# Two matmuls a token group in place of three for head scores and head values, in a two-layer transformer kernel

## What is computed

```python
def _L1_attn_ref(x, Wqkv, Wproj, bproj):
    qkv = jnp.einsum('bnm,fm->bnf', x, Wqkv).reshape(b, n, N_HEADS, -1)
    q, k, v = (qkv[..., :dh], qkv[..., dh:2 * dh], qkv[..., 2 * dh:])
    scores = jnp.einsum('bnhd,bngd->bnhg', q, k) / SCALE
    attn = jax.nn.softmax(scores, axis=-1)
    out = jnp.einsum('bnhg,bngd->bnhd', attn, v).reshape(b, n, -1)
    return jnp.einsum('bni,mi->bnm', out, Wproj) + bproj
```

## Time and profile before

| | us |
|---|---|
| three runs | 1480.59, 1487.53, 1486.54 |
| median | 1486.54 |
| profiled execution | 1478.55 |
| its span | 1476.6 |
| TensorE / VectorE / ScalarE / GpSimd busy | 1193.3 / 944.1 / 659.7 / 576.5 |
| mean granted clock of TensorE | 0.85 of full speed |

### The profile page before, as it was taken

How to read it: one execution, slowest core, us unless ns; L and a number is a source line. 1 busy time by engine, 2 the same in 40 slices (tenths; PEclk the granted TensorE clock), 3 DMA queues, 4 the chain that set the end, 5 groups by cost and what they waited for, 6 DMA issues and landing times.

```text
span 1476.6 us, 31197 instructions
## 1 busy us (share of the span) xinstructions
PE 1193.3 (81%) x12328; PEld 768.5 (52%) x12328; DVE 944.1 (64%) x2129; ACT 659.7 (45%) x1116; POOL 576.5 (39%) x888
## 2 busy tenths in 40 slices
PE   6678888988988888988979888988979877784443
PEld 3444555654655555554655565555655545442332
DVE  3444567586676767487667767487666777474524
ACT  3322472357424672357423762357423672356123
POOL 3125335335524534335524534334523515340312
PEclk8689996899879996899879986899879996797566
DMA  4000280207311280208320380208320290209120
GB/s 170 15 1 15 65 122 2 73 15 154 48 44 32 92 122 2 72 15 157 45 73 8 95 114 2 72 16 161 41 59 1 81 121 2 58 29 161 13 58 29
DMA packets 93017, 90.58 MB, mean 61 GB/s; under 512 B 7046, under 2 KB 81736, under 8 KB 92616
## 3 DMA queue, kind: packets, MB, share of 16 engines
q1 hardware_dynamic: 90312, 80.20, 28.3%
q0 software_dynamic: 2560, 8.39, 1.6%
HBM read 46.62 MB, written 41.94 MB: 60 GB/s over the span
## 4 chain that ended last, share of the span: by engine, by line
PE 41%; DVE 23%; POOL 9%; DMA 8%; issue 7%; ACT 7%; SPq 4%; POOLq 0%; DVEq 0%; ACTq 0%
PE bank L1468 39%; DVE blockdiag L1194 3%; POOL rs L517 3%; DVE keys L1259 3%; DMA bt<-scratch_o 3%; SPq L447 2%; DVE x L1167 2%; DVE gelu L1261 2%; DMA scratch_o<-stage 2%; DVE ct L1001 1%; ACT x L772 1%; DVE stats L1031 1%; DMA scratch_qkv<-part 1%; DMA scratch_qkv<-stage 1%; PE bank L1478 1%
## 5 line engine op out<-in xcount | busy, mean ns | idle before, releaser
L1468 PE MATMUL bank<-we,at 128*128 128x512 f16 x1536 | 368.8, 401 | 1.8 <-DVE x L1167 1.8
L1468 PEld LDWEIGHTS bank<-we,at 128*128 128x128 f16 x1536 | 154.7, 102 | 196.4 <-issue 40.7
L532 POOL TENSOR_TENSOR part<-part 128x512 f32<-128x512 f32 x64 | 82.9, 1295 | 283.0 <-ACTq L798 283.0
L667 ACT ACTIVATE part<-bank,wexp 128x256 f32<-128x256 f32 x256 | 105.2, 469 | 186.4 <-PE bank L1468 128.1
L1167 DVE SCALAR_TENSOR_TENSOR x<-bank,wexp,x 128x256 f32<-128x256 f32 x256 | 122.2, 477 | 72.6 <-PE bank L1468 66.6
L513 POOL TENSOR_SCALAR nm<-mv 128x2 f32<-128x2 f32 x128 | 32.2, 252 | 333.6 <-DVE mv L1036 329.1
L772 ACT ACTIVATE x<-x,nm,rs 128x256 f32<-128x256 f32 x192 | 104.6, 593 | 108.1 <-POOL nm L520 107.0
L1468 PE MATMUL bank<-bt,wqkv 128*128 128x512 f16 x576 | 137.5, 380 | 17.0 <-DVE stage L1001 13.3
L1001 DVE TENSOR_TENSOR stage<-bank,stage 128x512 f16<-128x512 f32 x112 | 75.4, 685 | 83.2 <-ACT stage L667 83.2
L667 ACT ACTIVATE stage<-bank 128x512 f16<-128x512 f32 x112 | 66.1, 597 | 126.8 <-PE bank L1468 73.6
L1468 PE MATMUL bank<-keys,blockdiag 128*128 128x16 f16 x3072 | 96.7, 193 | 26.9 <-DMA keys<-scratch_qkv 18.2
(11 more groups left out here) (177 smaller groups left out, 2241.0 us busy)
## 6 DMA issues: line engine op xcount, KB each, us to landing
scratch_qkv<-stage SPq DMA_DIRECT2D x40, 512.0 KB, 3.8
ct<-scratch_qkv SPq DMA_DIRECT2D x128, 128.0 KB, 6.0
x_in<-in_x_dram SPq DMA_DIRECT2D x32, 256.0 KB, 2.8
keys<-scratch_qkv SPq DMA_DIRECT2D x64, 128.0 KB, 5.4
scratch_o<-stage SPq DMA_DIRECT2D x64, 128.0 KB, 3.1
bt<-scratch_o SPq DMA_DIRECT2D x16, 512.0 KB, 3.8
out_dram<-x POOLq DMA_DIRECT2D x32, 256.0 KB, 2.6
scratch_qkv<-part SPq DMA_DIRECT2D x8, 512.0 KB, 8.4
```

Source lines behind the costliest of these rows:

```text
L532: pool.tensor_tensor(part[:, 0:2, :], part[:, 0:2, :], part[:, 2:4, :], ALU.add)\
L667: return act.activation(dst, src, ACT.Copy, scale=scale)
L1468: ins = pe.matmul(dst, lhs, rhs, start=(n == 0), stop=(n == len(terms) - 1))
```

## The change

- Each token group takes two matmuls in place of three: the HI matrix times 32 columns (HI and LO of keys or probabilities side by side), and the LO matrix times the 16 HI columns, added onto the first 16. A bank then holds two values a score, so quarters become eighths: S0 to S7 and O0 to O7, of 16 groups and 32 matmuls.
- VectorE evicts each of them with a `tensor_reduce` (add, pairs at a distance of 16) into half of `prob` (`b_s`, `b_o`). The maximum and the subtraction (`b_shift`) and the row sum (`b_ssum`) are functions of their own, over quarters, and now read `prob`.
- O's HI (ScalarE) and LO (VectorE, `b_olo`) are taken from `prob` in SBUF, 256 values each, in steps of 128 values, and no longer from PSUM.
- ScalarE makes 6 of V's 16 spreads, four of half 0 and two of half 1. VectorE makes the other ten, in five pieces placed at other points of its list.
- The order lists of all three engines are rewritten around that; ScalarE's normalisation `a_ln2n(b, 0)` comes ahead of the fourth exponent. SyncE's two waits ahead of the store become one. GpSimd's list is as it was.

```diff
+        def products(name):
+            return b_ps(name).rearrange("p (a l g) -> p a g l", l=2, g=H)
+        def prob_half(n):
+            return prob[:, n // 2 % 2, 256 * (n % 2):256 * (n % 2 + 1)]
+        def o_sum(n):
+            return prob_half(n).rearrange("p (c r h) -> p h r c", c=2, r=T)
 
...
-                sp.wait_ge(b_free[b_ring("O2")], b_read(b, "O2"))
-                sp.sem_inc(waits_held, 1)
-                sp.wait_ge(b_free[b_ring("O3")], b_read(b, "O3"))
+                sp.wait_ge(o_lo, 8 * (b + 1))
                 sp.sem_inc(waits_held, 1)
...
-            def b_o(b, q):
-                act.wait_ge(b_full, b_filled(b, f"O{q}"))
-                act.wait_ge(v_spread, 2 * b + 2)
-                copy(o_part(q, HI), o_psum(q)).then_inc(o_hi, 1)
+            def b_o(b, n):
+                for hf in range(2):
+                    act.wait_ge(v_spread[hf], 2 * (b + 1))
+                act.wait_ge(b_free[b_ring(f"O{n}")], b_read(b, f"O{n}"))
+                copy(o_part(n, HI), o_sum(n)).then_inc(o_hi, 1)
+            def b_spreadv(b, hf, rs):
+                act.wait_ge(v_turned, 2 * b + hf + 1)
+                act.wait_ge(b_full, b_filled(b, f"S{4 * hf + 3}"))
+                for r in rs:
+                    ins = copy(blockdiag[:, hf, :, DH * r:DH * (r + 1)], v_rows[hf], mask[:, r:r + 1])
+                if rs.stop == T:
+                    ins.then_inc(v_spread[hf], 1)
 
...
                 if c is not None:
                     b_s(c, 0)
                     b_s(c, 1)
+                    b_spreadv(c, 0, range(4, 6))
                 if b is not None:
                     a_moe(b, 2)
                 if c is not None:
                     b_pt(c, 0)
+                    b_spreadv(c, 0, range(6, T))
+                    b_pt(c, 1)
                     b_s(c, 2)
-                    b_pt(c, 1)
+                if b is not None:
+                    a_ln2n(b, 0)
+                if c is not None:
                     b_s(c, 3)
-                if b is not None:
-                    a_ln2n(b, 0)
+                    b_spreadv(c, 1, range(6, T))
+                if b is not None:
                     a_moe(b, 3)
                 if c is not None:
                     b_pt(c, 2)
                     b_pt(c, 3)
-                    b_o(c, 0)
-                    b_o(c, 1)
-                    b_o(c, 2)
-                    b_o(c, 3)
+                    for n in range(8):
+                        b_o(c, n)
...
-            def b_spreadv(b, hf, rs):
+            def b_spreadv(b, hf, rs, last=False):
 
                 dve.wait_ge(v_turned, 2 * b + hf + 1)
                 ins = spread(hf, v_rows[hf], rs)
-                if rs.stop == T:
-                    ins.then_inc(v_spread, 1)
-            def b_s(b, q):
-                dve.wait_ge(b_full, b_filled(b, f"S{q}"))
-                ps = b_ps(f"S{q}").rearrange("p (a g) -> p a g", g=H)
+                if last:
+                    ins.then_inc(v_spread[hf], 1)
+            def b_s(b, n):
+                dve.wait_ge(b_full, b_filled(b, f"S{n}"))
+                dve.tensor_reduce(prob_half(n).rearrange("p (a g) -> p a g", g=H), products(f"S{n}"), X, ALU.add)\
+                    .then_inc(b_free[b_ring(f"S{n}")], 1)
+            def b_shift(b, q):
+                for n in (2 * q, 2 * q + 1):
+                    dve.wait_ge(b_free[b_ring(f"S{n}")], b_read(b, f"S{n}"))
                 pr = prob[:, q % 2, :].rearrange("p (a g) -> p a g", g=H)
-                dve.tensor_reduce(smax[:, :], ps, X, ALU.max).then_inc(v_step_b, 1)
+                dve.tensor_reduce(smax[:, :], pr, X, ALU.max).then_inc(v_step_b, 1)
                 dve.wait_ge(v_step_b, done_b.next(b))
-                dve.tensor_tensor(pr, ps, smax[:, :, None].broadcast_to([P, 32, H]),
-                                          ALU.subtract).then_inc(b_free[b_ring(f"S{q}")], 1)
+                dve.tensor_tensor(pr, pr, smax[:, :, None].broadcast_to([P, 32, H]),
+                                  ALU.subtract).then_inc(s_shifted, 1)
+            def b_ssum(b, q):
+                pr = prob[:, q % 2, :].rearrange("p (a g) -> p a g", g=H)
                 dve.wait_ge(p_exp, 4 * b + q + 1)
                 dve.tensor_reduce(ssum[:, :], pr, X, ALU.add).then_inc(v_step_b, 1)
                 dve.wait_ge(v_step_b, done_b.next(b))
                 dve.wait_ge(pt_hi, 4 * b + q + 1)
                 split_lo(pt_part(q, LO), b_ps(f"PT{q}"), pt_part(q, HI)).then_inc(b_free[b_ring(f"PT{q}")], 1)
 
-            def b_o(b, q):
-                dve.wait_ge(o_hi, 4 * b + q + 1)
-                split_lo(o_part(q, LO), o_psum(q), o_part(q, HI)).then_inc(b_free[b_ring(f"O{q}")], 1)
+            def b_o(b, n):
+                dve.wait_ge(b_full, b_filled(b, f"O{n}"))
+                if n >= 4:
+                    dve.wait_ge(o_lo, 8 * b + n - 3)
+                dve.tensor_reduce(prob_half(n).rearrange("p (a g) -> p a g", g=H), products(f"O{n}"), X, ALU.add)\
+                    .then_inc(b_free[b_ring(f"O{n}")], 1)
+            def b_olo(b, n):
+                dve.wait_ge(o_hi, 8 * b + n + 1)
+                split_lo(o_part(n, LO), o_sum(n), o_part(n, HI)).then_inc(o_lo, 1)
 
...
                 if c is not None:
                     b_s(c, 0)
                     b_s(c, 1)
+                    b_shift(c, 0)
+                    b_s(c, 2)
+                    b_s(c, 3)
+                    b_ssum(c, 0)
+                    b_shift(c, 1)
+                    b_spreadv(c, 0, range(0, 2))
+                    b_ssum(c, 1)
                 if b is not None:
                     a_moe(b, 2)
+                if c is not None:
+                    b_pt(c, 0)
+                    b_s(c, 4)
+                    b_spreadv(c, 0, range(2, 4), last=True)
+                    b_s(c, 5)
+                    b_pt(c, 1)
+                    b_shift(c, 2)
+                if b is not None:
                     a_ln2(b, 0)
                 if c is not None:
-                    b_pt(c, 0)
-                    b_s(c, 2)
-                    b_spreadv(c, 0, range(T))
-                    b_pt(c, 1)
-                    b_s(c, 3)
+                    b_s(c, 6)
+                    b_ssum(c, 2)
+                    b_s(c, 7)
+                    b_shift(c, 3)
+                    b_spreadv(c, 1, range(0, 1))
+                    b_ssum(c, 3)
                 if b is not None:
                     a_moe(b, 3)
                 if c is not None:
                     b_pt(c, 2)
-                    b_spreadv(c, 1, range(T // 2))
                     b_pt(c, 3)
-                    b_spreadv(c, 1, range(T // 2, T))
+                    b_spreadv(c, 1, range(1, 4))
                     b_o(c, 0)
                     b_o(c, 1)
-                    b_o(c, 2)
-                    b_o(c, 3)
+                    b_spreadv(c, 1, range(4, 6), last=True)
+                    for n in range(2, 8):
+                        b_o(c, n)
+                        b_olo(c, n - 2)
+                    b_olo(c, 6)
+                    b_olo(c, 7)
...
+            key_pairs = keys[:, :, :].rearrange("p h (l t) -> p l h t", l=2)
+            def block(part, t, m):
+                return blockdiag[:, m // 8, 64 * part + 8 * t + m % 8, :]
+            def product(ps, n, part_of, pairs):
+                o = 2 * H * n
+                pe.matmul(ps[:, o:o + 2 * H], part_of(HI), pairs, start=True, stop=False)
+                return pe.matmul(ps[:, o:o + H], part_of(LO), pairs[:, HI, :], start=False, stop=True)
+            def b_s(b, n):
+                if n == 0:
                     pe.wait_ge(k_loaded, 16 * T * (b + 1))
-                pe.wait_ge(q_spread[q // 2], (1 + q // 2) * (b + 1))
-                pe.wait_ge(b_free[b_ring(f"S{q}")], b_before(b, f"S{q}"))
-                for c in range(4):
+                pe.wait_ge(q_spread[n // 4], (1 + n // 4) * (b + 1))
+                pe.wait_ge(b_free[b_ring(f"S{n}")], b_before(b, f"S{n}"))
+                for c in range(2):
                     for g in range(T):
-                        token = 16 * g + 4 * q + c
-                        n = T * c + g
-                        ins = sum_of(b_ps(f"S{q}")[:, H * n:H * (n + 1)],
-                                     [(block(q, i, g, c), keys[:, :, P * j + token])
-                                      for i, j in PASSES])
+                        ins = product(b_ps(f"S{n}"), T * c + g, lambda i: block(i, g, 2 * n + c),
+                                      key_pairs[:, :, :, 16 * g + 2 * n + c])
                 ins.then_inc(b_full, 1)
 
             def b_pt(b, q):
                                        prob[:, q % 2, P * c:P * (c + 1)], ident)
                 ins.then_inc(b_full, 1)
 
-            def b_o(b, q):
-                pe.wait_ge(v_spread, 2 * b + q // 2 + 1)
-                pe.wait_ge(b_free[b_ring(f"O{q}")], b_before(b, f"O{q}"))
-                pe.wait_ge(b_free[1 - b_ring(f"O{q}")], b_other(b, f"O{q}", (f"PT{q}",)))
```

(34 more changed lines are left out.)

16 lines of the change are left out of this document (6 added, 10 removed).

## The result

The changed kernel takes 1496.93 us (median of 4 runs, 1492.23 to 1497.88) against 1486.74 beside it (4 runs, 1480.59 to 1487.53): ratio 1.0072, 95% interval 1.0036 to 1.0108. On the chip of a later batch it was 1.0123 (1.0102 to 1.0144). The profiled execution took 1492.23 us, the fastest of the four, that of the kernel before 1478.55; their spans are 1490.3 and 1476.6.

What follows compares the result with a forecast made beforehand. No engine is full; VectorE's work up to the last low half of O was taken to set each turn. 7 x 1.3 + 1.7 = 10.8 us on the 1486.5 median gave 1497, range 1474 to 1518.

Steps and rivals of the forecast that it cites:

- The place: Scores to output projection: whatever moves the last low half of O moves the rest of the turn one for one.
- my sum: One full turn added step by step: 49.3 us against 48.0 before, 1.3 later; 11 us slower in all; chance 0.38.
- TensorE's saving: Scores and values: 6144 small matmuls become 4096, 7.6 us a turn at the lower bounds, cover and not path.
- The steps of the turn: Times after the scores' zero: low halves of PT0 17.3, PT1 21.8, PT3 35.9, the last 49.3 us.
- A piece of keys: Scores: one eighth, 32 matmuls, takes 1.3 us on TensorE, against 3.0 for a piece twice as large.
- A subtraction at 0.69: VectorE's shift of the scores: keeps its size and cost although it now reads SBUF.
- The collision that I charged to three spreads: Behind PT3: three VectorE spreads beside GpSimd's sum of block 3 lose 0.7 us, taking 2.9.
- The signs that I named: Trace checks: matmul counts, split near 0.59, PT1 4 to 5 us earlier; wrong if TensorE waits over 1 us in scores.
- Rival 2: Low halves of O: steps cost VectorE nothing, split 0.42, total 1 us more, 1487; chance 0.22.
- Rival 3: VectorE's queue: sums 0.62 apart, free steps, no collision; 2.8 us a turn, 22 us faster, 1464; chance 0.25.
- Rival 4: VectorE's subtraction and split, two SBUF operands, and GpSimd lock each other out: 27 us slower, 1513; chance 0.15.
- VectorE idle some 3 us before it: Ahead of PT3's low half at 35.9 us, 0.6 ahead of the kernel before, VectorE stands idle some 3 us.

Runs made afterwards that it cites:

- batch two: Later batch on one chip: the changed kernel, unedited, beside the kernel before, with variants; the unedited change took 1496.8 us, ratio 1.0123.
- e3: The changed kernel with a third matmul (LO times LO) added in each token group, 6144 small matmuls again: 1510.76 us, 1.0213 of the kernel before.
- e1: The changed kernel with O's groups reordered so the sum reads PSUM in steps and writes prob in order: 1485.25 us, 1.0049 of the kernel before.
- e8: e1 with ScalarE's last two V copies ahead of the fourth exponent and the normalisation behind it: 1465.56 us, 0.9914 of the kernel before.

## Why the prediction was right, point by point

Predicted 1497, measured 1496.9; direction and cause held. That it agrees to a tenth of a microsecond is chance: I forecast 10.8 more, the medians grew by 10.2 and the span of the traces by 13.7, and on the chip of batch two the change cost 18 us.

- **The place.** "What moves the last low half moves the rest of the turn one for one": stretches +13.4, span +13.7. Outside them, store to projection gave 1.8 back, projection to the next scores took 4.5, the start gave 2.6 back. Within the turn the place was right too: by my sum the change is 0.6 ahead at PT3 and loses 2.6 behind it against the trace, measured as 0.4 and 2.0 a turn (298.9 for 301.8, 103.5 for 87.1).
- **TensorE's saving is cover:** 31 us of busy time gone, and the time rose. e3 puts the limit: 61 us more of TensorE cost 14.5 us in the stretches, so a part would show if it were given back. The saving itself was sized too high: 3.9 us a turn (1193.3 to 1162.5) where my sum had 7.6 at the lower bounds, since the scores' products gave almost nothing (below). As cover it left the forecast alone.
- **The steps of the turn,** predicted and measured after zero: PT0's low half 17.3 and 18.4; PT1's 21.8 and 22.65; VectorE idle ahead of PT2's some 3 and 3.07; PT3's 35.9 and 36.6; the last 49.3 and 49.5. The durations: sum 0.69 and 0.68, split 0.59 and 0.60, high copy at most 0.63 and 0.65, the cadence of the two 1.12 and 1.11.
- **Terms mis-sized.** A piece of keys, 1.3, takes 1.40: the matmuls start some 44 ns apart, wide or narrow (0.2 us on the first two sums). A subtraction at 0.69 met GpSimd in this turn, 1.54 (0.85). These two make the 1.1 by which PT0 is late. The collision that I charged to three spreads late in the turn was smaller: they took 2.54 (588.95) where I had 2.9, with one of 1.22 among them. The lag falls from 1.1 at PT0 to 0.85 at PT1, 0.7 at PT3 and 0.2 at the last low half. Against the trace of before, the last low half is 2.2 later, not 1.3: my sum for the kernel before was 0.7 too late, and I compared with it. Three turns of eight lost as little as I said (1.1, 1.2 and 0.3), the others 1.8 to 2.6; the last, without expert blocks, 1.9 for my 1.7.
- **The signs that I named:** splits, sums, the 2048 matmuls each and VectorE's and ScalarE's busy times came as said. Three didn't. PT1's low half is 3.8 us earlier in place of 4 to 5. The last low half ends at 49.5, above the 48 to 49 that I wrote (my own sum had 49.3). And a sign of being wrong did come: in the scores TensorE waits 3.04 us for PT0's low half, which holds the bank of S5 (570.93). It cost nothing, since VectorE came to S5's sum behind two spreads and found it done (573.10, no wait).
- **Rival 2, steps free on VectorE,** falls by the row of 601 ns, and e1 shows what it would have been worth: 10.7 us of stretch, as it said 10. The Trainium skill, "Advanced Engine Details and Errata", section "SBUF Cachelines", gives a penalty for accesses that each fall on another 16-byte line, and the split's fall from 601 to 418 ns agrees. The Trainium skill, "VectorE: DVE Perf Modes", section "Mode 1× (REGULAR) — the baseline", counts odd strides among what works in this mode, one result a cycle; that they cost nothing doesn't hold for these reads.
- **Rival 3, the queue packs tighter:** sums stood some 0.6 apart where they followed one another directly, near the 0.62 it needed, but sum and split 1.11, and the steps weren't free. It fell with rival 2's condition. Its own sum was off as well: 1.7 + 1.3 + 0.7 + 0.7 less 1.3 is 3.1 a turn and not 2.8, so it should have stood 2 to 3 us lower. In the order of e8 something like it comes true (0.9914), by a hole that was closed, not by packing.
- **Rival 4, collisions,** exists and is small: subtraction 0.92 in the mean for 0.69, 32 x 0.23 = 7 us of VectorE's time over the whole kernel, not all of it on the path. A sentence of the Trainium skill, "SBUF — State Buffer", section "SBUF: two separate sides", that two SBUF inputs and a GpSimd instruction that reads SBUF shut one another out, agrees with 560.71 and 560.65, which ran side by side: the one took 1.54 for 0.69.

What I didn't see is the better reading of the same sum. Its own line "VectorE idle some 3 us before it" was a hole made by ScalarE's order, and moving two copies ahead of one exponent, and the normalisation behind it, was worth 19 us of stretch, more than the whole forecast. The same hole, by the rows, had room for the three spreads that VectorE makes behind PT3.

## What to carry to other kernels

Fewer matmuls buy nothing in a stretch that another engine's queue sets, and a product that needs a sum afterwards moves work onto that engine; price it there. Take a bundle apart before keeping or dropping it: here one part was worth 16 us and the rest cost more. When a part is judged, look at where in the turn its cost falls: it may be the order that came with it. Let the operation that has to reorder do it where it reads PSUM, so that later readers of SBUF go in order; and look at the holes in the deciding queue first, since closing one may cost a moved line.

## What the runs showed that I had not expected

- A matmul of 32 columns in 512-byte steps and the one of 16 columns behind it both start some 44 ns after the one before, a pair 88 ns against three of 31.5 (6.05 us over 192) = 94 before, or some 91 without the end of the last one: a third fewer matmuls saved 3 to 6%. With columns side by side a pair takes 60 ns (61.0 us over 1024) against 84. Why the narrow one is slow beside the wide one was not tried.
- An element-wise instruction pays for 512-byte steps in SBUF by 0.18 (VectorE) and 0.22 us (ScalarE) for 256 values, some 0.7 to 0.8 ns each; a sum that reads PSUM in like manner pays nothing (684 and 680 ns).
- The ratio of the same two kernels was 1.0072 on one chip and 1.0123 on another, intervals touching only barely, while the stretches differed by 1.3 us.
